# Moving the causal-mask multiplies to each query tile, and changing the waits at the hand-over to the feed-forward stage

## What is computed

```python
def reference(x, Wq, Wk, Wv, w1, b1, w2, b2, centroids, w_route):
    # x: (8, 4096, 1024); each core takes x[b]
    h = layernorm(x)
    q, k, v = h @ Wq.T, h @ Wk.T, h @ Wv.T
    s = q @ k.T / sqrt(1024);  s[j > i] = -inf          # causal
    x = x + softmax(s) @ v
    h = layernorm(x)
    logits = normalize(h) @ normalize(centroids).T + h @ w_route.T
    gates = softmax over the top 2 of 8 experts
    return x + sum_e gates[e] * (gelu(h @ w1[e] + b1[e]) @ w2[e] + b2[e])
```

## Time and profile before

| | |
|---|---|
| time of the kernel before, two runs | 2168.41 and 2169.88 us, median 2169.14 us |
| the profiled execution | 2171.88 us |
| its span on the slowest core (core 7) | 2170.3 us |
| spans of the eight cores | 2157.2 to 2170.3 us |
| granted TensorE clock, mean of a core | 0.936 to 0.938 of full |
| TensorE matmul busy | 1891.2 us (87%) |
| VectorE, ScalarE, GpSimd busy | 635.7, 496.6, 165.0 us |

### The profile page before, as it was taken

One profiled execution on the slowest core, in us unless ns is written; L12 is line 12 of the kernel. 1 busy time (PEld: TensorE's weight loads), 2 busy tenths in 40 slices (PEclk: granted clock), 3 DMA queues, 4 the chain that ended last, 5 costly groups with the idle time before them and its releaser, 6 DMA issues.

```text
span 2170.3 us, 32861 instructions; the slowest of 8 cores (2157.2 to 2170.3 us)
## 1 busy us (share of the span) xinstructions
PE 1891.2 (87%) x12448; PEld 1128.1 (52%) x12448; DVE 635.7 (29%) x1606; ACT 496.6 (23%) x1140; POOL 165.0 (8%) x193
## 2 busy tenths in 40 slices
PE   2999999655778898999947899999999999999998
PEld 2677777422333444444425466555566665556663
DVE  2232322155534425151342122222212222221220
ACT  1333333211122120303003122221222221112220
POOL 1111111011101101010020000000000000000000
PEclk9999999877888999999969999999999999999999
DMA  8312121133212212020179511111011111110110
GB/s 154 92 59 88 59 78 50 59 105 104 93 49 92 82 36 93 25 93 25 50 162 171 100 40 49 49 49 49 24 36 40 49 49 49 50 44 15 50 30 39
DMA packets 41163, 142.80 MB, mean 66 GB/s; under 512 B 4114, under 2 KB 4114, under 8 KB 37938
## 3 DMA queue, kind: packets, MB, share of 16 engines
q0 software_dynamic: 25552, 73.42, 13.7%
q1 hardware_dynamic: 15458, 67.28, 9.8%
HBM read 113.44 MB, written 50.33 MB: 75 GB/s over the span
## 4 chain that ended last, share of the span: by engine, by line
PE 76%; DVE 8%; DMA 8%; issue 5%; ACT 1%; another core or an unknown queue 1%; POOL 1%; DVEq 0%; SPq 0%; ACTq 0%; POOLq 0%
PE ph L950 22%; PE psc L588 11%; PE pout L854 10%; PE pout L856 10%; PE pqk L394 9%; PE pv L355 5%; PE pctx L638 4%; DMA x_scr<-x2b 3%; PE pctx L640 3%; DMA wqkv<-wvT 2%; DMA arena<-w1s 2%; DVE x2b L661 2%; DVE stt L664 1%; DVE xr L665 1%
## 5 line engine op out<-in xcount | busy, mean ns | idle before, releaser
L950 PE MATMUL ph<-ln2Tg,arena 128*128 128x256 bf16 x4096 | 483.4, 283 | 30.9 <-DMA arena<-w1s 27.5
L950 PEld LDWEIGHTS ph<-ln2Tg,arena 128*128 128x128 bf16 x4096 | 384.1, 101 | 132.0 <-issue 37.4
L970 ACT ACTIVATE hT<-ph,b_s 128x256 bf16<-128x256 f32 x512 | 242.9, 474 | 744.2 <-PE ph L950 744.1
L854 PE MATMUL pout<-arena,hT 128*128 128x512 bf16 x1024 | 389.4, 380 | 10.7 <-DMA b_s<-b 10.7
L856 PE MATMUL pout<-arena,hT 128*128 128x512 bf16 x1024 | 389.1, 380 | 0.0
L588 PE MATMUL psc<-qbuf,arena 128*128 128x512 bf16 x1152 | 270.0, 399 | 40.0 <-ACT probsT L601 31.5
L638 PE MATMUL pctx<-arena,probsT 128*128 128x512 bf16 x528 | 210.2, 398 | 56.6 <-DVE x2b L661 56.6
L979 DVE TENSOR_TENSOR hT<-hT,gbc 128x256 bf16<-128x256 bf16 x512 | 149.7, 292 | 361.6 <-ACT hT L970 361.6
L394 PE MATMUL pqk<-xlnT,wqkv 128*128 128x256 bf16 x2048 | 232.9, 275 | 16.3 <-ACT qstage L412 13.2
L394 PEld LDWEIGHTS pqk<-xlnT,wqkv 128*128 128x128 bf16 x2048 | 200.9, 99 | 49.0 <-issue 20.8
L588 PEld LDWEIGHTS psc<-qbuf,arena 128*128 128x128 bf16 x1152 | 116.1, 102 | 190.7 <-issue 69.2
(11 more groups left out here) (95 smaller groups left out, 1052.0 us busy)
## 6 DMA issues: line engine op xcount, KB each, us to landing
xbuf<-x SPq DMA_DIRECT2D x32, 512.0 KB, 4.0
xr<-x SPq DMA_DIRECT2D x32, 512.0 KB, 3.7
x_scr<-x2b POOLq DMA_DIRECT2D x32, 512.0 KB, 3.8
x2g<-x_scr SPq DMA_DIRECT2D x16, 1024.0 KB, 6.5
out<-outsb POOLq DMA_DIRECT2D x32, 512.0 KB, 2.9
qt_scr<-qstage POOLq DMA_DIRECT2D x16, 512.0 KB, 3.8
qbuf<-qt_scr SPq DMA_DIRECT2D x8, 1024.0 KB, 6.8
ln2t_scr<-ln2Ts POOLq DMA_DIRECT2D x32, 256.0 KB, 3.3
```

Source lines behind the costliest of these rows:

```text
L854: pe.matmul(pout[tl][:, 0:512], lhs, arena[:, b:b + 512], start=(hc == 0), stop=False)
L950: mm = pe.matmul(ph[hc % 2][:, 0:256], arena[:, kd * 4096 + hc * 128: kd * 4096 + hc * 128 + 128], ln2Tg[:, gc % 2, kd, :], start=(kd == 0 ...
L970: s.activation(hT[:, gc % 2, hc, :], ph[hc % 2][:, 0:256], AF.Gelu, bias=b1s[:, hc:hc + 1]))
```

## The change

Three places change. The mask multiply of key tile t is emitted at the head of iteration t of the tile loop, so that in VectorE's stream it stands behind all the work of iteration t-1. SP's gate waits for the last counts of ScalarE, VectorE and TensorE of the second stage. In the third stage the first gate transpose waits for VectorE's and ScalarE's last counts of the second stage, and the individual waits of pair 0's gate matmuls on `ln2T_cp[31]` and on the last exponential go.

```diff
-                def a2_ve_mask(v, g2=g2):
-                    for j in range(4 * g2, 4 * g2 + 4):
+                def emit_a2_mask(j, g2=g2):
+                    def a2_ve_mask(v, j=j, g2=g2):
                         off = (j - 4 * g2) * 128
                         v.wait_ge(sAc.h, V["exp_%d_%d" % (g2, j)])
                         mask_done[j] = sVe.inc(v.tensor_tensor(
                             probsT[:, j, off:off + 128],
                             probsT[:, j, off:off + 128],
                             cmask[:], ALU.mult))
-                blk.vector(a2_ve_mask)
+                    blk.vector(a2_ve_mask)
 
                 for tl in range(4):
                     t = 4 * g2 + tl
+                    emit_a2_mask(t)
...
             def c_sync_gate(sync):
-                sync.wait_ge(sPe.h, ctx_done[NT - 1])
+                sync.wait_ge(sAc.h, a2_ac_end)
+                sync.wait_ge(sVe.h, a2_ve_end)
+                sync.wait_ge(sPe.h, a2_pe_end)
...
                     if g == 0:
-                        pe.wait_ge(sVe.h, V["rtcp_%d" % (NT - 1)])
+                        pe.wait_ge(sVe.h, a2_ve_end)
+                        pe.wait_ge(sAc.h, a2_ac_end)
...
                         if pair == 0:
                             pe.wait_ge(sVe.h, V["gT2cp_%d" % gc])
-                            if gc == 0:
-                                pe.wait_ge(sVe.h, ln2T_cp[NT - 1])
                         if pair == 3:
                             pe.wait_ge(sVe.h, V["gbc_cp_%d_0" % gc])
-                        if gc == 0:
-                            if pair in (1, 2):
-                                pe.wait_ge(sAc.h, V["exp_7_31"])
-                        else:
+                        if gc >= 1:
```

## The result

The changed kernel takes 2378.77 us, median of 9 runs, against 2169.56 us before. The ratio is 1.0966, with a 95% interval of 1.0953 to 1.0979: clearly slower. The forecast was 2383 us in a range of 2350 to 2405.

What follows compares the result with a forecast made beforehand. TensorE was taken as the bound except between query tiles. Terms summed as 2171.9 + 150.2 + 6 + 48 + 9 = 2385 us, put at 2383 because the profiled execution lies 2.7 us above the median; range 2350 to 2405.

Steps and rivals of the forecast that it cites:

- The stall: Tile loops of groups 1 to 7: TensorE waits for the mask behind VectorE's work, 10.5 us per tile; +150.2 us.
- Group 0: First group's tile loop: smaller loss, as tiles 0 and 1 have no router work before the mask; +6 us.
- The clock: TensorE in groups 1 to 7: tiles begin at the 1.2 GHz level after each stall, 2.3 us a tile; +48 us.
- the rival of a clock that stays low: Tile loops: every matmul step at 1.2 GHz, 180 us and time 2515; half of it 2450; chance 0.04.
- SP's gate: Hand-over after tile 31: SP's four loads, 3.15 MB, move into the weight loads and delay their end; +9 us.
- The waits on TensorE: Third stage's start: first gate transpose waits for the last gates, hidden by the first w1 part; 0 us.

## Why the prediction was right

*The stall.* Right in kind and size. The forecast was that TensorE would start 11.9 us after x2b instead of 1.43; the tile of group 7 shown above has the mask ending at 1244.57, 11.64 us after x2b, TensorE starting at 11.9, and x2b of the next tile at 1261.26, a spacing of 28.3 us, where 26.8 plus a slow start were forecast. One detail was wrong: the transposes and router matmuls are not in the gap. They run ahead of x2b (1232.13 to 1232.93 in this tile), and the gap is empty. The loops of groups 1 to 7 were forecast at 54, 60, 65, 71, 76, 82 and 87 us and are 52, 61, 64, 70, 75, 82 and 87. Moving the mask back, ahead of the loop or behind x2b, takes all of it away, and the intermediate place gives an intermediate loss.

*Group 0.* +6 forecast, +4.6 measured.

*The clock.* +48 forecast, from four pieces of before with a mean of 2.3 us a tile. The loops of groups 1 to 7 are 42 us above the sum of stalls and matmuls at full clock; counting slow steps gives 37.6, and the filled gap took 40.6 us out of the loops. So the term was 6 to 10 us too large; it is 1.8 to 2.0 us a tile. The trace rows for a tile of the last group, the gap first:

```profile
1232.90:1244.80 11.90, 0.03 (x1) 0.70 0.35 110
1244.80:1247.30 2.50, 2.10 (x7) 0.50 0.00 0
1247.30:1249.80 2.50, 2.50 (x16) 0.87 0.04 7
1249.80:1260.50 10.70, 10.62 (x72) 1.00 0.00 0
```

The rule that I weighed against it, "the ramp penalty is <1% of a typical kernel span" (the Trainium skill, "TensorE: Matmul & The Clock Gate", Part 1), doesn't hold as a bound for this kernel: 38 us are 1.6% of its span, because the start is paid at every tile behind a stall. In the rival of a clock that stays low, half of the 180 us would give 2425 us and not 2450; nothing rests on it.

*SP's gate.* +9 forecast, and the run that has only the hand-over changes measured 9 (1.0042). The part behind x2b of tile 31 grew by 12.4 us on the cores shown and by 9.6 by the medians of all cores. What I had wrong is when: I gave the 8 to 10 us to the end of the weight queue and let the first expert block start on time, taking the one load of the earlier trace rows as the pattern. In fact the first w1 part was already 9.2 us late. Four loads back to back kept SP's queue filled, and it moved all its 3.15 MB within the first part's time (stretch 1310 to 1345):

```profile
q0 software_dynamic: 1888, 3.85, 76.7%
q1 hardware_dynamic: 576, 3.15, 26.7%
```

The window is 35 us long; up to the start of the first block, at 1335.8, GpSimd's queue had moved 2.51 MB and SP's all of its 3.15. The first part landed 29.9 us after its issue instead of 20.7, and the last 66.9 instead of 55.7, so the delay was there from the first part on and stayed about the same; that is why the sum wasn't touched.

*The waits on TensorE.* 0 forecast. In the run with SP's gate as before, where they are alone at the hand-over, the first block starts 0.75 us later than before with respect to x2b of tile 31. The 4 us that remain there behind x2b of tile 31 may or may not be theirs; it stays open whether 0 was right.

*What the sum left out.* The stretches between the loops became 3.6 us shorter. I had noted only that they were released by the same VectorE work.

*How much of the closeness is luck.* Groups 1 to 7 grew by 192 us where 150.2 + 48 = 198 were forecast. Without the 37.6 us of slow steps that leaves 155, so the stalls and matmuls were put 5 us too low and the clock 10 us too high. Part of the agreement to within 5 us is such errors cancelling; the range and the mechanism don't depend on it.

## What to carry to other kernels

When an instruction is moved within an in-order engine's stream, cost it by what stands in front of it at its new place, and ask who waits for it: a multiply of 0.22 us, moved behind 10 us of statistics, cost 10 us per tile because the bound engine needed its result. A stall on TensorE can cost more than its length: here every one of 4 us and more was followed by a slow start. It can pay to fill it, if the filling reaches close to the next real work: 1.08 us left was close enough, 4.1 us was not. And before moving a big load earlier, list what else goes through its queue: small stores behind it can inherit its whole time, 37.2 us here.

## What the runs showed of the hardware

- The price of a gap on TensorE hardly depended on its length. Slow steps in groups 1 to 7 summed to 37.6 us with gaps of 12 us, 40.5 us with gaps of 5 to 9, 39.7 us where the gap was filled but for its last 4.1 us, and 0.1 us where 1.08 us were left. Counted from the starts of the weight loads, the first three are 37.0, 39.9 and 37.4, so they can't be told apart. Over all eight cores of nine of the traces (groups 1 to 7; before, changed, and the runs on masks, gate, filling and the early store), none of the 425 tiles behind a gap of less than 1.5 us started slow, all 707 behind a gap of 4 us or more did, and of those between 1.5 and 3.9 us some did and some did not.
- In the gap of 12 us the granted clock fell within the gap (0.70 over it). In the gaps of 4.1 and 5.0 us it was 1.00 and 0.99 in the gap and 0.51 at the tile's start. The slow start cost about the same.
- In GpSimd's DMA queue a 512 KB store issued behind the 8 MB of w1 landed after 37.2 us; a 512 KB load alone in SP's queue at such a time landed in 10.3 us. With two stores ahead of it in SP's queue, one of them in 256 B packets, such a load landed after 25.4 us.
- A VectorE operation of 128x8 took 1.80 us instead of 0.23 beside a GpSimd operation of 128x1024, and ended 0.03 us after it.
- How much SP's queue moved beside the weights depended on what stood in it: with four loads waiting it moved 3.15 MB in 35 us in which GpSimd's queue moved 3.85 MB; with one load, 0.52 MB in 19 us.
